# Cross attention openings: first queries projected stacked, other queue orders, value products and the second half of queries inside steps 0 and 1

## What is computed

```
def cross_attention(query, context, mask, Wq, bq, Wkv, bkv, Wout, bout, num_heads):
    q = query @ Wq + bq
    kv = context @ Wkv + bkv
    ...                                    # 16 heads of 16
    scores = jnp.einsum('bhid,bhjd->bhij', q, k) * scale
    scores = jnp.where(mask[:, None, None, :], -jnp.inf, scores)
    attn = jax.nn.softmax(scores, axis=-1)
    out = jnp.einsum('bhij,bhjd->bhid', attn, v)
    return out @ Wout + bout
```

## Time and profile before

| | us |
|---|---|
| median of three runs | 1421.72 |
| profiled execution | 1429.85 |
| its span | 1427.6 |
| PE busy in the span | 1265.9 (89%) |
| DVE, ACT, POOL busy | 964.3, 760.1, 672.8 |
| first attention's first and fifth scores | 46.38, 60.99 |
| second attention's first and fifth scores | 788.39, 801.33 |
| one maximum (DVE, 128 x 1024), mean | 1.225 |
| one exponential (ACT, 128 x 1024), mean | 1.152 |
| one key cast (ACT) and one key rest (DVE), mean | 0.688, 0.750 |
| one value copy (ACT), mean | 0.588 |

### The profile page before, as it was taken

How to read it: one execution, slowest core, us unless ns; L and a number is a source line. 1 busy time by engine, 2 the same in 40 slices (tenths; PEclk the granted TensorE clock), 3 DMA queues, 4 the chain that set the end, 5 groups by cost and what they waited for, 6 DMA issues and landing times. The chain is left out here.

```text
span 1427.6 us, 34694 instructions
## 1 busy us (share of the span) xinstructions
PE 1265.9 (89%) x12166; PEld 1058.4 (74%) x12166; DVE 964.3 (68%) x1987; ACT 760.1 (53%) x1371; POOL 672.8 (47%) x602
## 2 busy tenths in 40 slices
PE   5799999999999688459996899999999997766787
PEld 3688888888887467358874788888888886555455
DVE  5577777777777565456406677777777776565995
ACT  2577777777776211012143677777777775123111
POOL 2556656656654223044232566566566653324341
PEclk9999999999999885569998899999999999868998
DMA  6677776776774220625537577767767762100000
GB/s 198 175 203 188 182 195 177 184 203 177 186 171 103 47 48 3 208 63 182 181 111 227 165 192 181 194 177 186 200 178 185 199 149 66 35 1 3 0 12 19
DMA packets 106724, 198.31 MB, mean 139 GB/s; under 512 B 43662, under 2 KB 63791, under 8 KB 106641
## 3 DMA queue, kind: packets, MB, share of 16 engines
q1 hardware_dynamic: 105104, 193.32, 51.3%
q0 software_dynamic: 1536, 3.88, 0.9%
HBM read 88.26 MB, written 10.62 MB: 69 GB/s over the span
## 5 line engine op out<-in xcount | busy, mean ns | idle before, releaser
L844 POOL TENSOR_SCALAR cross_prob<-cross_prob,cross_inverse 128x1024 f32<-128x1024 f32 x256 | 288.7, 1128 | 348.3 <-DVE cross_inverse L593 348.3
L771 ACT ACTIVATE cross_prob<-cross_negated,cross_negmax 128x1024 f32<-128x1024 f32 x256 | 294.9, 1152 | 148.7 <-DVE cross_negmax L585 148.4
L585 DVE CUSTOM_DVE_ANT_0 cross_negated<-cross_scores,cross_bias 128x1024 f32<-128x1024 f32 x256 | 313.6, 1225 | 31.1 <-PE cross_scores L476 13.7
L489 PE MATMUL cross_turn<-ident,cross_prob 128*128 128x128 f32 x2048 | 270.9, 275 | 14.9 <-POOL cross_prob L844 11.8
L489 PEld LDWEIGHTS cross_turn<-ident,cross_prob 128*128 128x128 f32 x2048 | 240.9, 142 | 54.7 <-POOL cross_prob L844 15.8
L780 ACT COPY cross_probT<-cross_turn 128x512 f32<-128x512 f32 x256 | 149.6, 584 | 68.7 <-PE cross_turn L489 67.6
L476 PE MATMUL cross_scores<-cross_keys,cross_qbd 96*128 96x512 f32 x512 | 169.9, 414 | 12.6 <-POOL cross_qbd L836 12.6
L601 DVE COPY cross_probT<-cross_turn 128x512 f32<-128x512 f32 x256 | 175.6, 686 | 5.5 <-PE cross_turn L489 5.5
L824 POOL TENSOR_TENSOR cross_ctx_lo<-cross_raw,cross_ctx_hi 128x512 fp32r<-128x512 f32 x120 | 156.0, 1302 | 24.6 <-ACT cross_ctx_hi L747 24.6
L419 PE MATMUL cross_out<-cross_wv_hi,cross_ctx_lo 128*128 128x256 f32 x488 | 147.9, 303 | 0.0
L421 PE MATMUL cross_out<-cross_wv_hi,cross_ctx_hi 128*128 128x256 f32 x488 | 137.7, 282 | 0.0
(11 more groups left out here) (269 smaller groups left out, 2061.4 us busy)
## 6 DMA issues: line engine op xcount, KB each, us to landing
cross_keys<-cross_key_hi SPq DMA_DIRECT2D x512, 128.0 KB, 2.3
cross_raw<-in_ctxT SPq DMA_DIRECT2D x32, 1024.0 KB, 5.6
cross_keys<-cross_key_lo SPq DMA_DIRECT2D x256, 128.0 KB, 2.4
cross_bias<-bias_rows SPq DMA_DIRECT2D x32, 512.0 KB, 3.6
up_sb<-in_moe_w SPq DMA_DIRECT2D x8, 1024.0 KB, 9.8
down_sb<-in_moe_w SPq DMA_DIRECT2D x8, 1024.0 KB, 11.6
cross_stacked_q<-q_rows SPq DMA_DIRECT2D x90, 64.0 KB, 2.0
q_rows<-cross_negated SPq DMA_DIRECT2D x8, 256.0 KB, 2.4
```

What stands on the lines that cost most here:

```text
L489: last = pe.transpose(ps_t[part][:, k * P:(k + 1) * P], prob[n % 2][:, kt * P:(kt + 1) * P], ident)
L585: dve.tensor_tensor_reduce(negated[n % 2], ps_s[n % 2][:, :], bias_sb[par][:, :], -1.0, 3.0e38, ALU.add, ALU.min, negmax[:, n % 2:n % 2 + ...
L771: act.activation(prob[n % 2][:, :], negated[n % 2], ACT.Exp, bias=negmax[:, n % 2:n % 2 + 1], scale=-1.0, accum_out=total[:, n % 2:n % 2 + ...
L844: pool.tensor_scalar(prob[n % 2][:, :], prob[n % 2][:, :], inverse[:, n % 2:n % 2 + 1], 1.0, ALU.mult, ALU.mult).then_inc(prob_ready, 1)
```

## The change

- PE makes the first batch's 64 queries in `project_first`: for each pair of heads, 32 columns of the query weights by 64 tokens, three times into partitions 0, 32 and 64 of the stacked layout (48 products of K = 128). `split_first` adds a stacked bias (`bq3`, a new small input) and makes hi and lo in place in `stacked_q`. The way through DRAM is left to the later batches.
- Statistics, roots, normalizing, transposes and copies go by pairs of tiles. The opening does pairs 0 and 1. Statistics of pairs 2 and 3 stand behind the query splits and ahead of the first maximum; they are normalized behind it, and transposed in step 1.
- The value pieces of batch 0 stand inside steps 0 and 1, two each, in the banks `proj` and `out`; query jobs 2 and 3 stand in step 1, their splits behind the maxima of steps 1 and 2.
- SP, first attention: half of x, identity and query weights ahead of key weights, context and value weights. Both: keys of pairs 0 to 3, the two stores, context 2, keys of pairs 4 to 7. Second: context 1 is loaded in `experts_block`.
- Second attention: for tiles 4 to 7 ScalarE scales the experts' rows (`weigh_taken`, 8 operations) and POOL adds them (`add_weighted`, 8); DVE keeps those of tiles 0 to 3.
- Context 2 is split in steps 4 to 7 of batch 0 instead of 1, 2, 5 and 6.

The diff, cut to its core:

```
-            sp.dma_start(t[:, :, :], self.w[k]).then_inc(self.w_loaded, 16)
-        sp.dma_start(self.raw[:, :, :], self.ctxT[0].rearrange("(g p) k -> p g k", p=P)).then_inc(self.ctx_loaded, 16)
+        sp.dma_start(self.wk[:, :, :], self.w["wk"]).then_inc(self.w_loaded, 16)
+        self.load_context(sp, 0)
+        sp.dma_start(self.wv[:, :, :], self.w["wv"]).then_inc(self.w_loaded, 16)
+
...
+        def split_steps(b):
+            return (4, 5, 6, 7) if is_first(b) else SPLIT_STEPS
...
                     sp.dma_start(out, in_).then_inc(masks_loaded, 16)
-                first.load_keys(sp)
-                for h in range(2):
-                    sp.dma_start(x[:, 4 * h:4 * h + 4, :], start["x"].rearrange("(h i p) d -> h p i d", h=2, p=P)[h]
-                                 ).then_inc(x_loaded[h], 16)
+                halves = [(x[:, 4 * h:4 * h + 4, :], start["x"].rearrange("(h i p) d -> h p i d", h=2, p=P)[h]) for h in range(2)]
+                sp.dma_start(*halves[0]).then_inc(x_loaded[0], 16)
                 sp.dma_start(ident, start["ident"]).then_inc(ident_loaded, 16)
                 sp.dma_start(half_mask[:, :], start["half_mask"]).then_inc(ident_loaded, 16)
                 first.load_queries(sp)
+                first.load_keys(sp)
+                first.load_rows(sp)
+                sp.dma_start(*halves[1]).then_inc(x_loaded[1], 16)
                 sp.wait_ge(masks_step, 3)
...
-            load_bias(1, 1)
-            sp.wait_ge(lo_done, 4)
-            load_ctx(1)
-            if taken is not None:
-                for g in range(G):
-                    first_keys(g)
-            for g in range(G):
-                store_queries(g, first_q_stored[g])
-            for g in range(G):
-                first_queries(g)
-                if taken is None:
-                    first_keys(g)
+            if start is not None:
+                sp.wait_ge(lo_done, 4)
+                load_ctx(1)
+            first_keys(0)
+            for n in range(G):
+                store_queries(n)
             sp.wait_ge(lo_done, 8)
             load_ctx(2)
+            first_keys(1)
             first.load_out(sp)
+            sp.wait_ge(q_stored, 32 * G)
+            load_bias(1, 1)
             sp.wait_ge(qbd_ready, G)
             load_queries(1)
             for n in range(G, len(q_jobs)):
-                store_queries(n, q_stored)
-            sp.wait_ge(q_stored, 32 * (len(q_jobs) - G))
+                store_queries(n)
+            sp.wait_ge(q_stored, 32 * len(q_jobs))
...
+            def project_first():
+
+
+                pe.wait_ge(copied, 1)
+                for n in range(PAIRS):
+                    for k in range(G):
+                        for part in range(3):
+                            last = pe.matmul(ps_s[1][32 * part:32 * part + 32, n * S:(n + 1) * S], wq[:, k, 32 * n:32 * n + 32],
+                                             xnT[:, k, 0:S], start=(k == 0), stop=(k == G - 1))
+                last.then_inc(first_projected, 1)
...
             if start is not None:
                 pe.wait_ge(ident_loaded, 32)
-                pe.wait_ge(q_loaded, 32)
+                pe.wait_ge(q_loaded, 48)
                 turn_tokens(0)
-                for n in range(G):
-                    project_queries(n)
-            for piece in range(1, 4):
-                project_key(0, 0, piece)
-            if start is None:
+                project_first()
+                for piece in range(2):
+                    project_key(0, 0, piece)
+            else:
+                for piece in range(4):
+                    project_key(0, 0, piece)
                 turn_tokens(0)
-                for n in range(G):
-                    project_queries(n)
-            for piece in range(4):
-                project_value(0, 0, piece)
+                project_first()
             turn_tokens(1)
-            for n in range(G, 2 * G):
+            for n in range(G):
                 project_queries(n)
+            if start is not None:
+                for piece in range(2, 4):
+                    project_key(0, 0, piece)
 
             def body(b, par):
                 for n in range(8):
                     scores(b, par, n)
                     two_before(turn, b, n)
+                    if is_first(b) and n < 2:
+                        for piece in (2 * n, 2 * n + 1):
+                            project_value(0, 0, piece)
+                    if is_first(b) and n == 1:
+                        for j in range(2, 4):
+                            turn_tokens(j)
+                        for job in range(G, 2 * G):
+                            project_queries(job)
                     project_at(b, par, n, project_key, project_value)
...
+            def pair(j):
+
+                for i in (2 * j, 2 * j + 1):
+                    if taken is not None and j < 2:
+                        add_taken(i, 0)
+                        add_taken(i, 1)
                     note(i)
                     aggregate(i)
...
+                normalize(0)
+                normalize(1)
+                split_first()
                 rest_key(0, 0, 0)
+                rest_key(0, 0, 1)
+            else:
+                rest_key(0, 0, 0)
+                normalize(0)
+                pair(1)
+                rest_key(0, 0, 1)
+                normalize(1)
+                split_first()
+                rest_key(0, 0, 2)
+                rest_key(0, 0, 3)
+            for n in range(G):
+                split_queries(n)
+            if start is not None:
+                rest_key(0, 0, 2)
...
-            split_queries(G)
+            pair(2)
+            pair(3)
 
...
-                            dve.wait_ge(first_q_stored[g], 32)
                     maxima(b, par, n)
                     if is_first(b) and n == 0:
+                        normalize(2)
+                        normalize(3)
+                    if is_first(b) and n == 1:
+                        split_queries(G)
+                    if is_first(b) and n == 2:
                         split_queries(G + 1)
...
+                round_key(0, 0, 3)
+            else:
+                split_hi(1, 1, 0)
+                split_hi(1, 1, 1)
+                act.wait_ge(rows_loaded, 48)
+                round_key(0, 0, 0)
+                split_hi(1, 1, 2)
+                round_key(0, 0, 1)
+                split_hi(1, 1, 3)
+                for i in range(4, 6):
+                    weigh_taken(i)
+                round_key(0, 0, 2)
                 copy_tokens(0)
-            for piece in range(1, 4):
-                round_key(0, 0, piece)
-            if start is None:
-                copy_tokens(0)
...
-                    if n in SPLIT_STEPS and not in_last(b, 2):
-                        split_hi(b + 2, par, SPLIT_STEPS.index(n))
+                    if is_first(b) and n < 2:
+                        for piece in (2 * n, 2 * n + 1):
+                            copy_value(0, 0, piece)
+                    if is_first(b) and n == 1:
+                        copy_tokens(2)
+                        copy_tokens(3)
+                    if n in split_steps(b) and not in_last(b, 2):
+                        split_hi(b + 2, par, split_steps(b).index(n))
             batches(act, body)
...
+                split_lo(1, 1, 0)
+                split_lo(1, 1, 1)
+                root(0)
+                split_lo(1, 1, 2)
+                root(1)
+                split_lo(1, 1, 3)
+                for i in range(4, 6):
+                    add_weighted(i)
+                for g in range(G):
+                    spread(0, 0, g)
+                for i in range(6, 8):
+                    add_weighted(i)
+                root(2)
+                root(3)
 
```

239 lines of the change are left out of this document (125 added, 114 removed).

## The result

The change made the kernel a little slower: 1430.62 us (median of 20 runs, 1426.23 to 1437.88) against 1424.93 of the kernel before in the same series (20 runs), **ratio 1.0036, 95% interval 1.0023 to 1.0049**, 5.7 us as the difference of the medians. The prediction had no change, 0.2 us less than before: 1421.5, within 1413 to 1430. It counted from 1421.72, the median of three runs; with twenty the kernel before stands at 1424.93. So of the 9.1 us between 1421.5 and 1430.62, 3.2 are the base and 5.9 the change; the time is 0.6 us above the range. The profiled executions are closer together, 1431.91 us (span 1430.1) against 1429.85 (1427.6): that of before was one of its longer ones. So I read places in the traces, not their ends.

The account below looks back on a forecast made before the run. PE was taken as the bound from the fifth step's scores on in each attention. 1.1 us late in the first and 1.3 early in the second sum to -0.2 us: 1421.5 us, within 1413 to 1430.

Parts of the forecast that it names:

- Removed with it: First attention: moving the splits to steps 4 to 7 removes ScalarE's 2.13 us wait for the context of batch 2.
- Behind it PE has no idle time: Both attentions, from the fifth step's scores on: PE stays busy, so time gained or lost earlier moves the end one for one.
- if PE idles in the steps behind the fifth scores: Sign that the forecast is wrong: PE idle there would mean the late splits of batch 2 are missed; no size given.
- the fifth scores: Start of the fifth step's scores: forecast 62.1 us in the first attention, 1.1 late, and 800.0 in the second, 1.3 early.
- Cast: First attention's opening: ScalarE first casts weights at 12.7 us, when both are there; ends 11.5 and 14.5.
- new product: The first queries' 48 small products, 96 rows: 2.9 us warm, 5.8 at half clock; 4.4 taken in the first attention.
- PE's stop: First attention, step 0: PE idles 3.2 us, with ScalarE's copy_value done at 42.8 us.
- Second attention: Sum for its opening: DVE sets the pace, first scores near 772.0 us, fifth scores at 800.0, 1.3 early.
- Term (f): First attention, step 0: DVE's statistics and first maximum, then ScalarE's exponential ahead of copy_value; 7.2 us, PE idles 3.2.
- DVE and POOL as the bound: Rival, both openings: DVE's work beside POOL sets the pace, adding 9 to 10 us, 1431 us; chance 0.12.
- Column groups one behind another: Rival, first queries' product: three column groups do not run side by side, 5.5 us for 2.9, 1426 us; chance 0.10.
- The idle time really filled: Rival, both openings: PE's waits are filled, gaining 3.5 us in the first attention, 5.5 in the second, 1412.5 us; chance 0.18.

Follow-up runs that it names:

- e1: Changed kernel with context 2 split in steps 1, 2, 5 and 6 of batch 0 again; 1426.47 us, ratio 1.0001.
- e2: Kernel before the change with only the splits of context 2 moved to steps 4 to 7 of batch 0; 1429.08 us, ratio 1.0019.
- e13: Changed kernel, late splits kept, with the 1 MB load of the fourth context cut to 16 numbers; 1426.88 us, ratio 1.0007.
- e8: Changed kernel with the second opening's eight weighted additions back on DVE, taken from ScalarE and POOL; 1433.05 us, ratio 1.0066.
- e7: Changed kernel with the statistics of the last four tiles of x behind the first maximum instead of ahead; 1431.32 us, ratio 1.0037.
- e3: Changed kernel with ScalarE's value copies of steps 0 and 1 ahead of the same step's exponential; 1427.42 us, ratio 1.0009.
- e10: Changed kernel with early splits, value copies first, value weights ahead, tokens 4 to 7 earlier, both late query splits in step 1; 1423.08 us, ratio 0.9986.
- e11: e10 with the late queries' four stores ahead of loading the second bias, batch 1's queries and output weights on SP; 1419.09 us, ratio 0.9942.

## Why the prediction was wrong

- **The step that failed** is the paragraph "Removed with it": the splits moved to steps 4 to 7, "its cover there is PE's own work", priced as a wait removed and nothing added; with it falls "Behind it PE has no idle time, and what is gained or lost ahead of it moves the end one for one". I asked who waits for the splits and not what is queued behind their end: the raw buffer is single, so the load of the next context starts with the last split, and ScalarE's next cast waits for it in order. It could have been read: before, that cast already waited 0.68 us, so there was no slack, and the load was issued 4.6 us later. The traces put it at 2.4 us, the ratios of e1, e2 and e13 at 5.0, 2.7 and 4.1, each known to 2 or 3. The prediction had named the sign ("if PE idles in the steps behind the fifth scores") and gave it no price.
- **The rest, no change, is right only as far as the medians tell:** 1.0001 with the splits back and 1.0007 with the wait away, each known to 0.12 to 0.18%. The traces have more: the fifth scores are 2.7 us late in sum where 0.2 early was forecast, and 1.2 us more are lost between them and batch 1. There PE stops for 0.27 us (63.62 and 804.46), for a copy that stands on ScalarE behind the one that waits for the stored queries. The rest of the 1.2 wasn't followed up.
- **First attention.** Cast 14.13 (12.7), new product 3.23 us (4.4), first scores 34.18 (35.6), PE's stop 3.29 us until 43.60 (3.2 until 42.8), fifth scores 62.72 (62.1). The mechanism was right; errors of 1.4 us cancelled, by luck. The new product was priced at 2.9 us at full clock, or 1.9 by columns alone; it took 1.99 (second attention), so the lower price was right.
- **Second attention.** It was to be 1.3 early at the fifth scores; from the block's own start it was 1.0 late (47.96 against 46.99 us). The miss is there when DVE starts the first maximum: 25.81 us of the block, where the sum has 23.3 (780.7 less 3.05 for maximum, exponential and copy, less 754.34). DVE ends the split of the first queries 1.2 us late (769.98 on the clock of before, not 768.8), and then it waits 1.43 us for the first query product, a wait that the sum doesn't have:

```profile
774.11 0.75 DVE L709 TENSOR_SCALAR result<-cross_scores,cross_bq 128x512 f32<-128x512 f32 x1 [1.43 <-PE cross_scores L551]
```

  The missed term in that wait is clock: I priced the two query products at 3.7 us, and they took 6.61 behind 2.29 us of idle time. That the first scores came at 776.33, not 772, matters less: in e1 and e13 they come 1.5 us sooner in the block, and the fifth scores at 48.00 and 47.96 all the same. The additions on POOL were rightly taken as a gain over DVE (e8).
- **Term (f)** named DVE's statistics and the first maximum. By the trace of e7 the statistics matter in the second attention (3.3 us at the fifth scores) and not in the first, where the tokens' chain is as late; e3 shows that the exponential ahead of copy_value does in part.
- **The rivals.** DVE and POOL as the bound (1431) gave nearly the time that came, mostly by luck: its 9 to 10 us lie ahead of the fifth scores, and these were only 2.7 us late in sum, though DVE's chain was 2.5 us late in the second attention; and POOL's additions are a gain. Column groups one behind another: no, 48 products took 1.99 us in the second attention, not 5.5, and doubling them cost nothing. The idle time really filled: only with e10 and e11 on top.
- **What a measurement can tell.** The prediction took 7 us. With twenty runs of each kernel the interval is 1.9 us to each side, so 5.7 us is clear of it.
- **How the slow rows vary.** The prediction said that the trace did not show it and cited the Trainium skill ("TensorE: Matmul & The Clock Gate", "Part 1") for it. The changed kernel, e8 and e13 issue the same instructions up to the third maximum of the first attention. It started at 56.51, 55.11 and 55.32 us with first casts at 14.13, 13.96 and 14.12, so up to 1.2 us apart from there on. The granted clock differs on the way: 0.50 of full from 44 to 48 us and 0.86 from 48 to 52 in the changed kernel, 0.57 and 1.00 in the other two.

## What to carry to other kernels

When a producer is moved to a later step, follow the buffer that it empties: the load that refills it moves as well, and on an engine that works in order the next reader blocks everything behind it, here a batch later than the place one looks at. A wait of 0.7 us for a load says that there is no slack to move anything ahead of it. Work put into idle time pays only when the chain that set the idle time (here normalize, transpose, copy, query, split, store) is moved with it; before that, three edits that took 5.0, 3.8 and 2.0 us off the changed kernel by themselves took off 5.1 together, which only made it level with the kernel before.

## What the runs showed of the hardware

- 48 fp32 products of 32 columns by 64 in three column groups (96 rows of the profile) take 1.99 us at full clock, 21 ns a row.
- The same 1 MB load took 6.2 us to land in the changed kernel, and 10.0 us in e11, with key transfers under way both times. What is planned to the microsecond behind a load isn't safe.
- A POOL power of 128x2 took 0.70 us where 128x4 took 1.01: half the elements save 0.31 us.
